# The first attention's bursts in a two-layer kernel: 69 bursts of two or three row pairs become 54 bursts of three pairs with a tail, and a group's maxima become ten packed pieces

## What is computed

```
x: (2, 512, 512), 32 heads of 16 channels, 8 key/value heads, so 4 query heads share one
xn = layernorm(x)
q, k, v = split(xn @ w_qkv); q, k = rope(q), rope(k)
scores = q k^T / 4, causal;  probs = softmax(scores);  out = (probs v) @ w_o
a = xn @ (gate_w * (gate_su @ gate_sv))^T ; b the same with up_*
x = x + out + (silu(a) * b) @ (down_w * (down_su @ down_sv))^T
```

## Time and profile before

| | us |
|---|---|
| median of 3 runs (lowest, highest) | 682.13 (681.68, 682.84) |
| profiled execution | 680.92 |
| its span in the trace | 679.2 |
| PE busy | 667.2 (98%) |
| DVE busy | 420.2 (62%) |
| ACT busy | 294.1 (43%) |
| POOL busy | 240.3 (35%) |

### The profile page before, as it was taken

One profiled execution on the slowest core, in us unless ns is written; L12 is line 12 of the kernel. 1 busy time (PEld: TensorE's weight loads), 2 busy tenths in 40 slices (PEclk: granted clock), 3 DMA queues, 4 the chain that ended last, 5 costly groups with the idle time before them and its releaser, 6 DMA issues.

```text
span 679.2 us, 9978 instructions
## 1 busy us (share of the span) xinstructions
PE 667.2 (98%) x3518; PEld 507.2 (75%) x3518; DVE 420.2 (62%) x987; ACT 294.1 (43%) x557; POOL 240.3 (35%) x242
## 2 busy tenths in 40 slices
PE   8997999999999999999999999999999999999998
PEld 7785666666666666666687778888888788888886
DVE  6956867676776676665367665378565665646501
ACT  4324355555545455455434415344444444343321
POOL 4595122223312222222323626803232243323443
PEclk9998999999999999999999999999999999999999
DMA  8448425231322222221145520500010011112011
GB/s 296 136 146 219 103 58 129 77 77 47 77 77 77 77 77 62 77 79 49 47 142 161 192 90 1 158 1 32 31 32 32 31 62 33 31 32 70 9 63 62
DMA packets 23145, 55.17 MB, mean 81 GB/s; under 512 B 3732, under 2 KB 4088, under 8 KB 22040
## 3 DMA queue, kind: packets, MB, share of 16 engines
q1 hardware_dynamic: 22840, 54.41, 27.4%
q10 hardware_dynamic: 256, 0.13, 0.1%
HBM read 42.86 MB, written 11.54 MB: 80 GB/s over the span
## 4 chain that ended last, share of the span: by engine, by line
PE 91%; DVE 2%; POOL 2%; DMA 1%; ACT 1%; issue 1%; SPq 1%; DVEq 0%; ACTq 0%
PE bank L52 25%; PE bank L54 23%; PE bank L53 23%; PE bank L1062 6%; PE bank L1097 5%; PE bank L1084 3%; PE bank L180 2%; PE bank L1070 1%; DMA wqkv_raw<-in_w_qkv 1%; PE bank L344 1%; PE bank L108 1%; POOL wqkv_lo L528 1%; DMA q_stack<-minus_max_rows 1%; PE bank L1654 1%; DVE lrd L141 0%
## 5 line engine op out<-in xcount | busy, mean ns | idle before, releaser
L1008 DVE CUSTOM_DVE_ANT_0 bank<-bank,mask 128x512 f32<-128x512 f32 (+3 forms) x256 | 118.4, 523 | 59.8 <-PE bank L1062 59.5
L217 POOL TENSOR_TENSOR up_w_lo<-up_w_eff,up_w_hi 128x512 fp32r<-128x512 f32 x50 | 65.9, 1323 | 105.6 <-ACT up_w_hi L213 105.5
L52 PE MATMUL bank<-x0T_hi,up_w_hi 128*128 128x512 f32 x224 | 96.9, 432 | 3.1 <-DVE up_gated L284 3.1
L382 POOL TENSOR_TENSOR down_h_lo<-hidden,down_h_hi 128x512 fp32r<-128x512 f32 x50 | 66.1, 1324 | 88.4 <-ACT down_h_hi L377 88.3
L962 ACT ACTIVATE probs<-bank 128x512 f32<-128x512 f32 x160 | 85.0, 598 | 27.8 <-PE bank L1084 25.2
L54 PE MATMUL bank<-x0T_lo,up_w_hi 128*128 128x512 f32 x224 | 89.5, 400 | 0.0
L53 PE MATMUL bank<-x0T_hi,up_w_lo 128*128 128x512 f32 x224 | 89.3, 399 | 0.0
L927 POOL TENSOR_SCALAR_AFFINE_SELECT probs<-probs 128x512 f32<-128x512 f32 x64 | 39.9, 635 | 118.8 <-ACT probs L962 118.8
L52 PE MATMUL bank<-down_w_hi,down_h_hi 128*128 128x512 f32 x200 | 78.5, 393 | 0.4 <-DVE bind_cols L1374 0.4
L53 PE MATMUL bank<-down_w_hi,down_h_lo 128*128 128x512 f32 x200 | 78.0, 390 | 0.0
L377 ACT ACTIVATE down_h_hi<-hidden 128x512 fp32r<-128x512 f32 x50 | 31.6, 631 | 91.5 <-PE bank L54 91.5
(11 more groups left out here) (166 smaller groups left out, 1362.9 us busy)
## 6 DMA issues: line engine op xcount, KB each, us to landing
w_raw<-in_w_gate_up SPq DMA_DIRECT2D x25, 512.0 KB, 3.3
w_raw<-in_w_down SPq DMA_DIRECT2D x25, 256.0 KB, 3.0
q_stack<-q_hi SPq DMA_DIRECT2D x32, 128.0 KB, 3.5
att<-att_T SPq DMA_DIRECT2D x16, 256.0 KB, 2.0
q_hi<-rope_hi SPq DMA_DIRECT2D x8, 256.0 KB
q_lo<-rope_lo SPq DMA_DIRECT2D x8, 256.0 KB
q_stack<-q_lo SPq DMA_DIRECT2D x16, 128.0 KB, 3.6
attention_or_xn<-att SPq DMA_DIRECT2D x16, 128.0 KB
```

The lines of the kernel that those rows point to most:

```text
L52: pe.matmul(out, w_hi, m_hi, start=first, stop=False, skip_group_check=True)
L217: pool.tensor_tensor(self.half(self.w_lo[:, o % 2], k), self.half(self.w_eff, k), f32(self.half(self.w_hi[:, o % 2], k)), ALU.subtract).th ...
L382: pool.tensor_tensor(self.h_lo[:, k % 2, :], self.hid[:, o, b * S:(b + 1) * S], f32(self.h_hi[:, k % 2, :]), ALU.subtract).then_inc(self.h ...
L1008: dve.tensor_tensor_reduce(out=own, in0=own, in1=e.mask[:, S - w:S], scale=1.0, scalar=NEG, op0=ALU.add, op1=ALU.max, accum_out=rmax[:, i, ...
```

## The change

A burst now always holds up to three maxima pieces and up to three key pieces, and runs on across the borders of groups. Maxima piece number n of the whole sequence (ten to a group, 160 in all) goes into burst n // 3, and the key piece of the same number into burst n // 3 + 5 (`LAG`). Bursts 0 to 53 hold maxima, 54 to 58 keys alone (54 with the last low transposes, 55 with values), 59 the last values, and burst 60 has no work for PE but SP's last store. Bursts follow steps 6 + 31 m // 9, every third or fourth step. High transposes come one burst after a group's eighth maxima piece, low ones one after its tenth, values one after its tenth key piece. The stack of group g + 4 is loaded in the burst of the values of g.

The maxima are packed into ten pieces: four of 512, four of 384 + 128, two of 256 + 256 columns. So that keys of the next group may start before the values of this one, odd groups write their first two key pieces into a buffer of their own, `probs_more`, and their values read these with 8 separate matmuls; `exp_piece` waits accordingly. `rows_of` stays as it is.

```diff
...
-LEAD, EVERY = 4, 3
-MAX_PIECES = [(3, h, 1) for h in range(4)] + [(2, h, 1) for h in range(4)] + [(1, 0, 2), (1, 2, 2), (0, 0, 4)]
-MAX_END = [1, 2, 3, 4, 5, 6, 7, 8, 10, 12, 16]
-MAX_BURST = [(0, 2), (2, 5), (5, 8), (8, 11)]
+MAX_PIECES = [[(3, h)] for h in range(4)] + [[(2, h), (0, h)] for h in range(4)] + [[(1, 0), (1, 1)], [(1, 2), (1, 3)]]
+MAX_END = [1, 2, 3, 4, 6, 8, 10, 12, 14, 16]
+MAX_HIGH = 8
 KEY_PIECES = [(j, i) for i in (3, 2, 1, 0) for j in range(i + 1)]
-KEY_BURST = [(0, 2), (2, 5), (5, 8), (8, 10)]
-KEYS = len(KEY_PIECES)
+KEYS, WIDTH, LAG = len(KEY_PIECES), 3, 5
 BLOCK_OF = {(j, i): sum(NJ - m for m in range(j)) + i - j for j, i in KEY_PIECES}
-HIGH_AT, LOW_AT = 3, 1
-BURSTS = 4 * (GROUPS + 1)
+EARLY = KEY_PIECES[0:2]
+
+
+class Burst:
+
+
+    def __init__(self):
+        self.maxima, self.keys = [], []
+        self.high = self.low = self.values = self.store = self.load = None
+
+
+def bursts_of_groups():
+
+    end = (KEYS * GROUPS - 1) // WIDTH + LAG + 2
+    bursts = [Burst() for _ in range(end + 1)]
+    for g in range(GROUPS):
+        for p in range(KEYS):
+            at = (KEYS * g + p) // WIDTH
+            bursts[at].maxima.append((g, p))
+            bursts[at + LAG].keys.append((g, p))
+            if p == MAX_HIGH - 1:
+                bursts[at + 1].high = g
+        bursts[at + 1].low = g
+        bursts[at + LAG + 1].values = g
+        bursts[at + LAG + 2].store = g
+        if g + 4 < GROUPS:
+            bursts[at + LAG + 1].load = g + 4
+    return bursts
+
+
+BURSTS = bursts_of_groups()
+BURST_AFTER = {6 + 31 * m // 9: m for m in range(len(BURSTS))}
 
 
 def burst_after(step):
-
-    t, left = divmod(step - LEAD, EVERY)
-    return t if left == EVERY - 1 and 0 <= t <= BURSTS else None
+    return BURSTS[BURST_AFTER[step]] if step in BURST_AFTER else None
 
 
 def factor_before(step):
 
     o, r = divmod(step, 16)
-    first = (EVERY - 1 + LEAD - 16 * o) % EVERY
-    return (o + 1, (r - first) // EVERY) if o + 1 < CH0 and r in (first, first + EVERY) else None
+    places = (0, 3) if o == 0 else sorted(at % 16 for at in BURST_AFTER if at // 16 == o)[0:2]
+    return (o + 1, places.index(r)) if o + 1 < CH0 and r in places else None
...
-            if burst_after(step) is not None:
-                s = stages_of(burst_after(step))
-                if s["high"] is not None:
-                    narrow.place(("minus_max", s["high"], 1), neg_copied, 2 * s["high"] + 1)
-                if s["low"] is not None:
-                    narrow.place(("minus_max", s["low"], 0), neg_copied, 2 * s["low"] + 2)
-                if s["values"] is not None:
-                    narrow.place(("values", s["values"]), att_out, s["values"] + 1)
-                if s["maxima"] is not None:
-                    for p in range(*MAX_BURST[s["at"]]):
-                        wide.place(("maxima", s["maxima"], p), reduced, NJ * REP * s["maxima"] + MAX_END[p])
-                if s["keys"] is not None:
-                    for p in range(*KEY_BURST[s["at"]]):
-                        narrow.place(("keys", s["keys"], p), exp_done, KEYS * s["keys"] + p + 1)
+            burst = burst_after(step)
+            if burst:
+                if burst.high is not None:
+                    narrow.place(("minus_max", burst.high, 1), neg_copied, 2 * burst.high + 1)
+                if burst.low is not None:
+                    narrow.place(("minus_max", burst.low, 0), neg_copied, 2 * burst.low + 2)
+                if burst.values is not None:
+                    narrow.place(("values", burst.values), att_out, burst.values + 1)
+                for g, p in burst.maxima:
+                    wide.place(("maxima", g, p), reduced, NJ * REP * g + MAX_END[p])
+                for g, p in burst.keys:
+                    narrow.place(("keys", g, p), exp_done, KEYS * g + p + 1)
...
-                if burst_after(step) is not None and burst_after(step) % 4 == 0:
-                    n = burst_after(step) // 4
-                    if 2 <= n <= GROUPS:
-                        store(n - 2)
-                    if 3 <= n + 2 < GROUPS:
-                        load_stack(sp, n + 2)
-            store(GROUPS - 1)
+                burst = burst_after(step)
+                if step == min(BURST_AFTER):
+                    load_stack(sp, 3)
+                if burst and burst.store is not None:
+                    store(burst.store)
+                if burst and burst.load is not None:
+                    load_stack(sp, burst.load)
+
+        def probs(g, j, i):
+
+            return e.probs_more[:, EARLY.index((j, i))] if g % 2 and (j, i) in EARLY else pt[:, BLOCK_OF[j, i], :, :]
 
         def gpsimd(pool):
...
             def exp_piece(g, p):
                 act.wait_ge(s2_mm, KEYS * g + p + 1)
-                if p == 0 and g >= 1:
+                if p == 0 and g >= 2:
+                    act.wait_ge(pv_mm, g - 1)
+                if p == len(EARLY) and g >= 1:
                     act.wait_ge(pv_mm, g)
-                act.activation(pt[:, BLOCK_OF[KEY_PIECES[p]], :, :],
+                act.activation(probs(g, *KEY_PIECES[p]),
                                narrow.bank(("keys", g, p))[:, :].rearrange("p (h s) -> p h s", h=REP),
...
                 K = slice(r, r + STK - 1)
-                i, h, nh = MAX_PIECES[p]
                 wide.free(pe, ("maxima", g, p))
-                w = (i + 1) * P
                 bank = wide.bank(("maxima", g, p))
-                for n in range(nh):
-                    last = pe.matmul(bank[:, n * w:(n + 1) * w], qst[K, slot, h + n, i * P:(i + 1) * P], kst[K, slot, 0:w],
-                                     start=(n == 0), stop=(n == nh - 1), skip_group_check=True)
+                at = 0
+                for i, h in MAX_PIECES[p]:
+                    w = (i + 1) * P
+                    last = pe.matmul(bank[:, at:at + w], qst[K, slot, h, i * P:(i + 1) * P], kst[K, slot, 0:w],
+                                     start=(at == 0), stop=((i, h) == MAX_PIECES[p][-1]), skip_group_check=True)
+                    at += w
                 last.then_inc(s1_mm, 1)
...
                 for j in range(NJ):
-                    own = slice(BLOCK_OF[j, j], BLOCK_OF[j, j] + NJ - j)
+                    apart = g % 2 and (j, NJ - 1) in EARLY
+                    count = NJ - j - 1 if apart else NJ - j
+                    own = slice(BLOCK_OF[j, j], BLOCK_OF[j, j] + count)
                     for h in range(REP):
-                        last = pe.matmul(bank[32 * h:32 * (h + 1), j * P:], e.v[:, b, j, kv, :], pt[:, own, h, :],
+                        last = pe.matmul(bank[32 * h:32 * (h + 1), j * P:(j + count) * P], e.v[:, b, j, kv, :], pt[:, own, h, :],
                                          start=(j == 0), stop=(j == NJ - 1), skip_group_check=True)
+                    if apart:
+                        for h in range(REP):
+                            pe.matmul(bank[32 * h:32 * (h + 1), (NJ - 1) * P:], e.v[:, b, j, kv, :], probs(g, j, NJ - 1)[:, h, :],
+                                      start=False, stop=False, skip_group_check=True)
                 last.then_inc(pv_mm, 1)
 
             for step in range(STEPS):
...
-                if burst_after(step) is not None:
-                    s = stages_of(burst_after(step))
-                    if s["high"] is not None:
-                        minus_max(s["high"], 1)
-                    if s["low"] is not None:
-                        minus_max(s["low"], 0)
-                    if s["values"] is not None:
-                        values(s["values"])
-                    first, count = MAX_BURST[s["at"]][0], max(b - a for a, b in (MAX_BURST[s["at"]], KEY_BURST[s["at"]]))
-                    for n in range(count):
-                        if s["maxima"] is not None and first + n < MAX_BURST[s["at"]][1]:
-                            max_scores(s["maxima"], first + n)
-                        if s["keys"] is not None and KEY_BURST[s["at"]][0] + n < KEY_BURST[s["at"]][1]:
-                            key_scores(s["keys"], KEY_BURST[s["at"]][0] + n)
+                burst = burst_after(step)
+                if burst:
+                    if burst.high is not None:
+                        minus_max(burst.high, 1)
+                    if burst.low is not None:
+                        minus_max(burst.low, 0)
+                    if burst.values is not None:
+                        values(burst.values)
+                    for n in range(WIDTH):
+                        if n < len(burst.maxima):
+                            max_scores(*burst.maxima[n])
+                        if n < len(burst.keys):
+                            key_scores(*burst.keys[n])
...
+            with ExitStack() as to_down0:
+                e.probs_more = holder(to_down0, "left")("probs_more", [P, len(EARLY), REP, P])
```

More of the change, by code:

```diff
@@ L829, in rows_of @@
             return 64 * (g % 2), (g // 2) % 2
-        def stages_of(t):
-            n, k = divmod(t, 4)
```

(27 more changed lines are left out.)

53 lines of the change are left out of this document (26 added, 27 removed).

## The result

The changed kernel takes **697.12 us** (median of 4 runs, 695.88 to 697.62) against 682.25 us before: ratio 1.0216, 95% interval 1.0203 to 1.0228, or 14.9 us slower. The forecast was 694.4 us in a range of 689.5 to 700.0. In the experiments, two single executions of 2140 and 3674 us are left out of the medians.

The account below looks back on a forecast made before the run. PE, busy for 98% of the span, was taken to bound the kernel. The terms -3.5 + 16.8 - 4.1 + 1.2 + 1.5 + 0.9 - 0.5 gave +12.3 us on 682.13: 694.4 us, range 689.5 to 700.

Parts of the forecast that it names:

- Fewer bursts: On PE, 60 bursts instead of 69, each saving 0.39 us: -3.5 us.
- Pairs in one half: On PE, 70 of 145 maxima and key pairs share an array half and must queue, so their maxima are paid: +16.8 us.
- Packing: On PE, four lone 128-column maxima per group go (-6.1 us), packed pieces run slightly longer (+2.0): together -4.1 us.
- Ends and counts: On PE, different numbers of maxima alone, keys alone and pairs before and after: +1.2 us.
- Values: On PE, odd groups add 8 values matmuls at equal total width; bounds 0 to 2.5 us, taken as +1.5 us.
- Waits: PE's bank waits: low bursts -2.6 us, third key behind values +3.0, high bursts and masks +0.5: together +0.9 us.
- The start: Burst 0's third piece falls into PE's idle 3.13 us; the first key no longer waits for its DMA: -0.5 us.
- the first (halves don't matter): PE runs same-half pairs like opposite ones, so 16.8 us fall away: -4.5 us, 677.6 us; chance 0.05.
- The second, ACT setting the pace: In the narrow ring, 40 bursts each lose 0.33 us to ACT, 13.2 in place of 3.5: 704.1 us; chance 0.08.
- The third, weight loads bared in one half: On PE, 0.18 us loads exposed twice in each of 70 same-half pairs: +25 us, 719.6 us; chance 0.01.
- the fourth, slack: Stage has hidden slack, such as maxima slipping beside neighbouring keys; at most half the same-half cost: 686 us; chance 0.04.

Follow-up runs that it names:

- the kernel before by one line: Kernel before, with groups placed in array halves by twos (0, 1 low, 2, 3 high) instead of by parity, nothing else changed: 696.46 us, ratio 1.0204.
- a short copy: Changed kernel, with ACT copying only 128 of 512 columns of the attention values of groups 2 to 15: 694.5 us, ratio 1.0172.

## Why the prediction was right, and where its sum was off

The direction, its cause and the size hold; the sum was 2.6 us short by the medians (12.3 for 14.9) and 3.6 us by the two traces (12.3 for the stage's 15.9). The steps are read from the traces. Within the bursts the sum says 12.8 us (all terms but the start) and 13.2 were measured. That this is so close is in part luck: the pairs and the values were priced too high, the waits too low, and the errors cancel. By its steps:

- **Fewer bursts**, -3.5 us. Right. Three keys alone still cost 1.08 us, and PE has 60 bursts. No run shows the saving as a whole, since no version with 60 or 62 bursts got rid of what comes with them.
- **Pairs in one half**, +16.8 us. Right in mechanism, shown in the kernel before by one line (+14.2 us) and in burst 7 (0.21 us a pair in place of 0.24). The step took the price as paid in every burst. In bursts with high and low transposes ACT's copies set the time either way, so that there it was the longer of two, and not a sum. Bursts of one kind with and without their pairs in one half (1.46 and 1.20 us, 1.61 and 1.15, 1.56 and 1.37, 1.77 and 1.38, 2.01 and 1.37, 2.52 and 2.51) give an estimate of 12 us for the 70 pairs.
- **Packing**, -4.1 us within the bursts. Right where it was measured (1.48 to 1.08 and 1.09 to 1.20 us), but the kernel with packing alone shows what the step left out: the values wait for POOL, and DVE falls behind at the start. In the changed kernel the first comes to 1.4 us in three waits, and the second is the start below.
- **Ends and counts**, +1.2 us. Not measured apart.
- **Values**, +1.5 us. Wrong: nothing. The last values, alone in their burst, run from 345.84 to 348.14 us, 2.30 us. The last values before, undivided, run from 330.29 to 332.58 us, 2.29 us. Before and after:

```profile
330.29 2.36 PE L1097 MATMUL bank<-probs,v_ones 128*32 128x512 f32 x32
332.58 0.50 PE L344 MATMUL bank<-lrd 96*128 96x512 f32 x1
```

```profile
345.84 0.85 PE L1120 MATMUL bank<-probs,v_ones 128*32 128x384 f32 x8
346.51 0.40 PE L1124 MATMUL bank<-probs_more,v_ones 128*32 128x128 f32 x8
...
347.38 0.83 PE L1120 MATMUL bank<-probs,v_ones 128*32 128x256 f32 x16
348.14 0.50 PE L52 MATMUL bank<-x0T_hi,up_w_hi 128*128 128x512 f32 x1
```

  The distance of starts would have said so, durations of matmuls in flight do not. The Trainium skill's page TensorEngine Tiling (Array Packing), section Instruction Overhead, which the prediction weighed, says that a matmul shorter than some 60 cycles is no faster. By that a split into 384 and 128 columns is free, and the measurement agrees. The narrow maxima are not priced by their columns alone: a packed piece beside its key costs 0.04 us more (1.19 us for three pairs in place of 1.08), though its columns are as many.
- **Waits**, +0.9 us. Too low. The third key behind values was right as a mechanism: -2.6 us with a short copy. Its size was more: 3.70 us in nearly all of the fifteen bursts is 0.32 us above 3.15 and a third pair at 0.23, not 0.2 us. The low bursts did lose their waits. The five bursts with both transposes were passed over. With all pairs opposite they still cost 2.51 us, where three pairs and two kinds of transposes come to 1.08 + 2 x 0.29 = 1.66: 0.85 us each is the wait for the banks that ACT's two copies empty. From these figures an estimate of all waits is 15 x 0.32 - 2.6 + 5 x 0.85 = 6.5 us, with the pairs beneath them counted as free.
- **The start**, -0.5 us. This step failed. It saw a gain where burst 0 fits into idle time, and said of DVE that its idle 30% covers the packed pieces. That share is a mean over the stage. From 64 to 68 us DVE is busy for 3.9 of 4 us in both kernels, and in the earlier trace rows the gate was already what PE waited for, and the low-rank factors and the next gate stand behind the maxima on its queue. PE lost 1.2 us in two waits and about as much to the slow clock behind them: measured +2.4 us by the product of step 24, with the bursts up to there as long as before. That is 2.9 us more than the step said, most of the 3.6 us that the sum was short. Mending it in the changed kernel gave back 1.4 us in the trace.

Of the rivals, the first (halves don't matter) fell with the one-line change in the kernel before. The second, ACT setting the pace, is true in part: not in 40 bursts, but in the third keys behind values and the five bursts with both transposes, and it caps what mending the halves can give. The third, weight loads bared in one half, fell with burst 7: each load lies under the matmul ahead, six at 0.23 us. So did the fourth, slack: none of the six slips beside another.

## What to carry to other kernels

When two streams of small matmuls share the array by row halves, a new lag between them is first a question of which half each partner then lies in; write down the pairs for one period before counting bursts. Price a step that frees a resource by what waits for it next: here packing freed 0.4 us a group on PE, and the next mask took most of it back, until the order of the key pieces was changed too. And a mean idle share covers nothing at a stage's start, where one late instruction costs its wait and can cost a stretch at the lower clock behind it. An edit that ends one wait there has to be checked against the trace: in three of the four kernels with an early gate or early factors another wait stood in its place.

## What the runs showed of the hardware

Two matmuls in opposite halves start together (94.10 and 94.10 above) or within 0.12 us and cost one; in one half they follow at 0.23 us for 512 columns, with the next one's weights (a load of 0.18 us) loaded meanwhile. Going from full-row passes into the half-row mode and back costs about 0.38 us beyond the matmuls, an estimate: 1.08 us less three times 0.233. PE's idle time of 1.2 us in two waits near 74 us was followed by a stretch at 1.2 GHz from about 76.5 to 80 us, after some 1.6 us at 2.4 GHz. It was there too behind waits of 1.8 and of 1.9 us, and not in the kernel with both factors and gate early, which has no such wait. But behind the 1.12 us of the kernel with the longer lag and the copies first it was not there either. What decides it stays open.
